# A four-block transformer kernel: bf16 queries by ScalarE, two single turns of maxima, an earlier load, idle matmuls at the first score, new order tables

## The reference, cut to what matters

```python
x = L0(x): x + g*attn(ada_ln(x)), self attention with rotary q and k and a mask
           x + g*attn(ada_ln(x), context), key mask
           x + g*mlp(ada_ln(x))            # 128 -> 512 -> 128, gelu
x = L1(x): x + attn(ada_ln(x), ada_ln(context))
x = L2(x): x + g*attn(ada_ln(x)); x + attn(ln(x), context); x + g*mlp(ada_ln(x))
x = L3(x): q = ln(x) @ Wq; evidence = softmax(q k / sqrt(128)) v   # one head
           three experts and a gate over [ln(x), evidence, anchor]
# attention: 16 heads of 8 channels
s = einsum('bqhd,bkhd->bhqk', q, k) / sqrt(8); a = softmax(s); o = a @ v
```

## Time and profile before

| | |
|---|---|
| runs, median | 585.58 us (580.8 to 586.85) |
| profiled execution, its time | 584.01 us |
| its span, first to last instruction | 581.9 us |
| mean granted TensorE clock | 0.974 |
| TensorE busy | 541.6 us, 93% |
| TensorE weight loads busy | 336.1 us, 58% |
| VectorE busy | 384.7 us, 66% |
| ScalarE busy | 319.7 us, 55% |
| GpSimd busy | 336.2 us, 58% |

### The profile page before, as it was taken

The page is one execution under the profiler, slowest core; times in us unless marked ns, Lnnn a source line. Parts: engine busy times, 40 slices in busy tenths (PEclk is TensorE's granted clock), DMA queues, the critical chain, the costliest instruction groups (busy, mean ns, idle before and its releaser), DMA issues.

```text
span 581.9 us, 17488 instructions
## 1 busy us (share of the span) xinstructions
PE 541.6 (93%) x7121; PEld 336.1 (58%) x7126; DVE 384.7 (66%) x1062; ACT 319.7 (55%) x523; POOL 336.2 (58%) x424
## 2 busy tenths in 40 slices
PE   7799889999899999999999989998999999997996
PEld 3354445556455675556565645655668647775565
DVE  4847788976878577867688568789727513635124
ACT  2004256454655856674757575665746669444671
POOL 3372874582979757886688785778747302343000
PEclk9757899999999999999999999999999999999999
DMA  7810200010100010001000000000000000000000
GB/s 254 289 51 4 75 21 3 4 37 2 37 3 21 3 37 2 21 2 38 2 13 10 20 20 3 3 7 15 5 17 2 2 2 1 19 19 0 1 2 37
DMA packets 17818, 16.07 MB, mean 28 GB/s; under 512 B 4333, under 2 KB 15863, under 8 KB 17483
## 3 DMA queue, kind: packets, MB, share of 16 engines
q1 hardware_dynamic: 16875, 10.82, 6.3%
q10 hardware_dynamic: 864, 4.13, 1.9%
HBM read 13.85 MB, written 1.09 MB: 26 GB/s over the span
## 4 chain that ended last, share of the span: by engine, by line
PE 61%; DVE 8%; ACT 6%; issue 5%; POOL 2%; POOLq 0%; DVEq 0%; ACTq 0%
PE ring L1074 16%; PE ring L1086 13%; PE big L1175 10%; PE ring L1208 8%; DVE mhl L891 3%; ACT P L655 3%; PE ring L1151 3%; PE big L1192 2%; PE ring L1096 2%; PE ring L1081 2%; DVE bst L827 1%; ACT hT L633 1%; POOL xn L547 1%; DVE oT L932 1%; PE ring L1140 1%
## 5 line engine op out<-in xcount | busy, mean ns | idle before, releaser
L891 DVE TENSOR_REDUCE mhl<-ring 128x4 bf16<-128x308 f32 (+1 forms) x320 | 163.9, 549 | 39.3 <-PE ring L1151 30.5
L655 ACT ACTIVATE P<-big 77x1024 f32<-77x1024 f32 (+1 forms) x128 | 124.6, 1019 | 104.0 <-PE big L1192 103.4
L547 POOL TENSOR_SCALAR xn<-x,mv,rstd 128x128 f32<-128x128 f32 x124 | 100.2, 822 | 3.2
L562 POOL TENSOR_TENSOR kbm<-kT,hm 128x308 bf16<-128x308 f32 (+1 forms) x80 | 69.2, 870 | 56.3 <-DVE kT L875 22.2
L575 POOL TENSOR_TENSOR qm<-qT,hm 128x512 f32<-128x512 f32 x80 | 83.7, 1051 | 25.3 <-PE big L1192 21.0
L1175 PE MATMUL big<-qm,kT 32*77 32x512 f32 (+1 forms) x640 | 91.5, 630 | 3.3 <-ACT P L655 2.8
L1074 PE MATMUL ring<-hT,W 128*128 128x512 f32 x176 | 90.0, 616 | 4.2 <-ACT hT L633 3.0
L1208 PE MATMUL ring<-P,Vp 77*32 77x128 f32 (+1 forms) x2560 | 86.5, 275 | 4.3 <-DVE mhl L891 1.2
L1208 PEld LDWEIGHTS ring<-P,Vp 77*32 77x32 f32 (+1 forms) x2560 | 65.6, 109 | 25.2 <-issue 15.6
L633 ACT ACTIVATE hT<-ring,tab 128x128 f32<-128x128 f32 x96 | 36.1, 460 | 52.7 <-PE ring L1096 52.3
L1086 PEld LDWEIGHTS ring<-W,hid 128*128 128x128 f32 x480 | 57.4, 192 | 2.8 <-issue 2.0
(11 more groups left out here) (169 smaller groups left out, 734.8 us busy)
## 6 DMA issues: line engine op xcount, KB each, us to landing
gring<-gate_rows SPq DMA_DIRECT2D x20, 256.0 KB, 3.5
W<-in_w ACTq DMA_DIRECT2D x1, 2624.0 KB, 15.0
hid<-in_ws SPq DMA_DIRECT2D x1, 1536.0 KB, 12.2
x<-in_x SPq DMA_DIRECT2D x4, 256.0 KB, 4.6
out<-x SPq DMA_DIRECT2D x4, 256.0 KB, 2.0
W<-in_w ACTq DMA_DIRECT2D x1, 768.0 KB, 6.8
ctxT<-in_ctxT SPq DMA_DIRECT2D x4, 154.0 KB
ctx<-in_ctx SPq DMA_DIRECT2D x4, 154.0 KB
```

The lines of the kernel that those rows point to most:

```text
L547: i = nc.gpsimd.tensor_scalar(dst[0:t, b, :], src[0:t, b, :], mv[s][0:t, o, b, 0:1], rstd[s][0:t, o, 1, b:b + 1], ALU.subtract, ALU.mult)
L562: nc.gpsimd.tensor_tensor(kbm[:, j % 2, :, 0:kw], k.broadcast_to([128, 4, kw]), mask.broadcast_to([128, 4, kw]), ALU.mult).then_inc(kbm_re ...
L655: nc.scalar.activation(P[0:kw, j % 2, 8 * half:8 * half + 8, :], big[0:kw, 2 * half:2 * half + 2, :].rearrange("p g (h q) -> p (g h) q", h=4),
L891: v.tensor_reduce(mhl[:, j // 2 % 2, c:c + 4], at(item)[:, 0:4 * kw].rearrange("p (h k) -> p h k", h=4), AX, ALU.max).then_inc(free(item), 1)
```

## The change

- `p{a}:qc:s` leaves VectorE. For attentions 1 to 4, ScalarE's item `p{a}:q:s` now makes two copies from the projection's bank: first `qb` in bf16, then `qT` in f32, which frees the bank. For attention 0 ScalarE gets an item `p0:qc:s`, a copy of `qT` to `qb` behind the rotation.
- `SINGLE = 2`: the maxima of jobs 0 and 1 are turned each by itself (`tu:0`, `tu:1`), those of later jobs in pairs as before. The halves of `mhl` and `mt` go by the number of the turn.
- x of group 1 is loaded behind the identity, ahead of the masks, and its statistics stand ahead of the first rotation.
- `PE_IDLE`: 20 idle matmuls at `s:0:0`, 11 instead of 21 at the first transposes, none at `p0:v:0`, others at items of jobs 0 to 5.
- All four tables are new; the modulation columns are spread among the first scores, the signs stand ahead of the first normalisation, and elsewhere items move by a place or two.

```diff
-u:g0:0=1 u:g1:0=1 s:0:1=1 s:0:3=1 s:1:3=1 s:2:2=2 l0:t:0=21 p0:v:0=5 p0:k:1=1
+u:mc:0=1 s:0:0=20 s:0:3=4 s:1:2=3 s:2:0=1 s:3:0=3 s:3:1=1 s:3:3=1 av:3=1 s:5:0=1 s:5:2=2 l0:t:0=11 p0:v:1=1
...
 PE_ORDER = program("""
-l0:t:0 p0:q:0 p0:k:0 p0:v:0 s:0:0 s:0:1 s:0:2 s:0:3 s:1:0 s:1:1 u:ma:0 u:mb:0 u:mc:0 u:mods:0 s:1:2 s:1:3 s:2:0 st:0
-s:2:1 s:2:2 tu:0 l0:t:1 su:0 s:2:3 s:3:0 s:3:1 p0:q:1 u:g0:0 p0:k:1 s:3:2 s:3:3 st:1 u:g1:0 su:1 av:0 p0:v:1 tu:2 st:2
...
+l0:t:0 p0:q:0 p0:k:0 p0:v:0 s:0:0 s:0:1 s:0:2 u:ma:0 s:0:3 s:1:0 s:1:1 s:1:2 u:mb:0 tu:0 s:1:3 s:2:0 st:0 su:0 s:2:1
+s:2:2 u:mc:0 l0:t:1 tu:1 u:mods:0 st:1 su:1 s:2:3 s:3:0 s:3:1 p0:q:1 p0:k:1 st:2 s:3:2 s:3:3 av:0 p0:v:1 u:g0:0 tu:2
+su:2 av:1 u:g1:0 s:4:0 s:4:1 st:3 su:3 s:4:2 s:4:3 s:5:0 s:5:1 av:2 av:3 s:5:2 s:5:3 u:bias:0 tu:4 st:4 su:4 s:6:0
...
 DVE_ORDER = program("""
-l0:stat:0 first:0 l0:a:0 first:1 first:2 p0:qa:0 p0:ka:0 p0:k:0 p0:q:0 p0:qc:0 p0:v:0 mx:0:0 mx:0:1 mx:0:2 mx:0:3
-mx:1:0 mx:1:1 l0:stat:1 u:mc:0 u:ma:0 u:mb:0 u:mods:0 mx:1:2 l0:stat:2 mx:1:3 mx:2:0 mx:2:1 tr:0 mx:2:2 mx:2:3 mx:3:0
...
+l0:stat:0 first:1 l0:a:0 first:0 first:2 l0:stat:1 p0:qa:0 p0:ka:0 p0:k:0 p0:q:0 p0:v:0 mx:0:0 mx:0:1 u:ma:0 mx:0:2
+mx:0:3 mx:1:0 mx:1:1 mx:1:2 tr:0 u:mb:0 l0:stat:2 mx:1:3 mx:2:0 mx:2:1 mx:2:2 l4:stat:0 u:mc:0 tr:1 u:mods:0 mx:2:3
...
 ACT_ORDER = program("""
-l0:t:0 l0:t:1 ex:0:0 ex:0:1 ex:1:0 ex:1:1 ex:2:0 ex:2:1 ex:3:0 ex:3:1 ex:4:0 p1:k:0 ex:4:1 ex:5:0 ex:5:1 l0:t:2 l1:t:0
...
+l0:t:0 p0:qc:0 ex:0:0 ex:0:1 l0:t:1 ex:1:0 ex:1:1 p0:qc:1 ex:2:0 ex:2:1 ex:3:0 ex:3:1 ex:4:0 ex:4:1 l0:t:2 p1:k:0
...
 POOL_ORDER = program("""
-l0:r:0 kb:0 kb:1 kb:2 qm:0 l0:a:1 qm:1 kb:3 l0:a:2 qm:2 kb:4 kb:5 qm:3 l4:a:0 qm:4 kb:6 nm:0 kb:7 qm:5 l0:a:3 qm:6
...
+l0:r:0 kb:0 qm:0 kb:1 qm:1 kb:2 l0:a:1 kb:3 l0:a:2 qm:2 kb:4 kb:5 qm:3 kb:6 qm:4 nm:0 qm:5 kb:7 qm:6 l0:a:3 l1:a:0
...
+SINGLE = 2
...
 def pair_of(j):
 
-    return j - j % 2
+    return j if j < SINGLE else j - j % 2
+
+
+def pair_last(j):
+    return j if j < SINGLE else pair_of(j) + 1
...
+TURNS = list(dict.fromkeys(pair_of(j) for j in range(JOBS)))
+
+
+def turn_of(j):
+    return TURNS.index(pair_of(j))
...
             sp.dma_start(ident[:], ident_in).then_inc(ident_ld, 16)
+            sp.dma_start(xs[1][:], x_in[:, GB:2 * GB, :]).then_inc(x_in_s[1], 16)
             for c in range(4):
...
-            for s in range(1, NS):
+            for s in range(2, NS):
                 sp.dma_start(xs[s][:], x_in[:, s * GB:(s + 1) * GB, :]).then_inc(x_in_s[s], 16)
...
             def project(a, s, part):
                 A, item = ATT[a], (f"p{a}", part, s)
+                if part == "qc":
+                    act.wait_ge(rope_q[s], 1)
+                    nc.scalar.activation(qb[s][:], qT[s][:], ACT.Identity).then_inc(qb_ready[s], 1)
+                    return
+                if part == "q":
+
+                    full(act, item)
+                    kw = {"bias": c_(A["bq"])} if A["bq"] else {}
+                    nc.scalar.activation(qb[s][:], at(item), ACT.Identity, **kw).then_inc(qb_ready[s], 1)
                 dst, n, bias = (qT, N, A["bq"]) if part == "q" else (kT, GB * A["kw"], A["bk"])
...
-            def cast(a, s):
-                if a == 0:
-                    dve.wait_ge(rope_q[s], 1)
-                else:
-                    taken(dve, (f"p{a}", "q", s))
-                v.tensor_copy(qb[s][:], qT[s][:]).then_inc(qb_ready[s], 1)
...
-                if g == 0 and j >= 4:
+                if g == 0 and turn_of(j) >= 2:
 
-                    full(dve, ("tu", pair_of(j) - 4))
+                    full(dve, ("tu", TURNS[turn_of(j) - 2]))
...
-                taken(pe, ("s", j + 1, 3))
+                taken(pe, ("s", pair_last(j), 3))
```

More of the change, by code:

```diff
@@ L104 @@
[L104 to L108, removed]
@@ new lines @@
+s:37:2 st:35 su:35 s:37:3 s:38:0 av:34 tu:36 s:38:1 s:38:2 st:36 su:36 av:35 s:38:3 s:39:0 l1:t:3 s:39:1 s:39:2 st:37
+s:39:3 su:37 av:36 p1:q:3 av:37 l4:t:2 tu:38 st:38 s:40:0 s:40:1 s:40:2 su:38 s:40:3 s:41:0 o2:y:1 l2:t:2 s:41:1
+s:41:2 st:39 s:41:3 su:39 av:38 m0:h0:2 m0:h1:2 m0:h2:2 m0:h3:2 p1:v:3 tu:40 av:39 m0:y:2 st:40 s:42:0 s:42:1 su:40
+s:42:2 o3:y:0 p4:k:0 p2:k:2 st:41 s:42:3 su:41 s:43:0 s:43:1 s:43:2 s:43:3 av:40 l3:t:2 tu:42 st:42 su:42 p2:q:2
+p2:v:2 av:41 s:44:0 s:44:1 l5:t:1 s:44:2 s:44:3 st:43 s:45:0 su:43 s:45:1 s:45:2 s:45:3 av:42 l6:t:0 tu:44 av:43
@@ L194 @@
-x3:r2:2 x3:e0:2 x3:r2:3 x3:e1:2 x3:e0:3 x3:e1:3 x3:e2:3 x3:y:3 x3:e2:2 x3:y:2
+l0:stat:0 first:1 l0:a:0 first:0 first:2 l0:stat:1 p0:qa:0 p0:ka:0 p0:k:0 p0:q:0 p0:v:0 mx:0:0 mx:0:1 u:ma:0 mx:0:2
+mx:0:3 mx:1:0 mx:1:1 mx:1:2 tr:0 u:mb:0 l0:stat:2 mx:1:3 mx:2:0 mx:2:1 mx:2:2 l4:stat:0 u:mc:0 tr:1 u:mods:0 mx:2:3
+mx:3:0 p0:qa:1 mx:3:1 p0:ka:1 mx:3:2 p0:k:1 mx:3:3 p0:q:1 tr:2 t1:0 p0:v:1 u:g0:0 l0:stat:3 u:g1:0 t1:1 mx:4:0 mx:4:1
+mx:4:2 mx:4:3 mx:5:0 t1:2 mx:5:1 t1:3 nr:0 mx:5:2 mx:5:3 nt:0 tr:4 u:bias:0 mx:6:0 mx:6:1 o0:y:0 l1:stat:0 mx:6:2
@@ new lines @@
+mx:6:3 mx:7:0 mx:7:1 t1:4 mx:7:2 mx:7:3 t1:5 tr:6 l4:stat:2 l4:stat:3 p1:v:0 l4:stat:1 mx:8:0 mx:8:1 mx:8:2 mx:8:3
+mx:9:0 t1:6 mx:9:1 mx:9:2 mx:9:3 t1:7 mx:10:0 tr:8 mx:10:1 mx:10:2 mx:10:3 nr:1 mx:11:0 mx:11:1 mx:11:2 p0:ka:2
+mx:11:3 p0:k:2 tr:10 t1:8 p0:qa:2 p0:q:2 t1:9 p0:v:2 nt:1 mx:12:0 mx:12:1 mx:12:2 mx:12:3 mx:13:0 t1:10 mx:13:1
+mx:13:2 t1:11 mx:13:3 nr:2 mx:14:0 tr:12 o0:y:1 nt:2 l1:stat:1 mx:14:1 mx:14:2 o1:y:0 mx:14:3 mx:15:0 mx:15:1
+l2:stat:0 t1:12 mx:15:2 mx:15:3 tr:14 t1:13 mx:16:0 mx:16:1 mx:16:2 mx:16:3 p1:v:1 mx:17:0 mx:17:1 mx:17:2 mx:17:3
@@ L234 @@
+qm:73 l7:a:1 nm:17 qm:74 kb:75 kb:76 l6:a:3 kb:77 qm:75 qm:76 l8:a:0 qm:77 kb:78 kb:79 qm:78 l8:a:1 nm:18 qm:79 l7:a:2
+nm:19 l7:a:3 l8:a:2 l8:a:3
 """)
@@ L895, in turn @@
                 item = ("tu", j)
-                if j >= 4:
-                    dve.wait_ge(st_full, 2 * (j - 3) + 2)
+                if turn_of(j) >= 2:
+                    dve.wait_ge(st_full, 2 * pair_last(TURNS[turn_of(j) - 2]) + 2)
                 full(dve, item)
-                v.tensor_copy(mt[:, j // 2 % 2, :], at(item).bitcast(BF16)[:, 0:T]).then_inc(free(item), 1)
+                v.tensor_copy(mt[:, turn_of(j) % 2, :], at(item).bitcast(BF16)[:, 0:T]).then_inc(free(item), 1)
             def unload(j):
@@ L1026, in _ @@
                     norm(int(st[1:]), item[2])
-                elif part == "qc":
-                    cast(int(st[1:]), item[2])
                 elif st == "p0" and part in ("q", "k"):
@@ L1180, in turn @@
                 take(item)
-                taken(pe, ("s", j + 1, 3))
+                taken(pe, ("s", pair_last(j), 3))
                 hold(pe)
-                give(item, nc.tensor.transpose(at(item).bitcast(BF16)[:, 0:T], mhl[:, j // 2 % 2], identb[:]))
+                give(item, nc.tensor.transpose(at(item).bitcast(BF16)[:, 0:T], mhl[:, turn_of(j) % 2], identb[:]))
             def subtract(j):
```

216 lines of the change are left out of this document (103 added, 113 removed).

## The result

The changed kernel took 582.78 us (median; 575.94 to 590.86) against 585.03 of the kernel before in the same sessions: ratio 0.9933, 95% interval 0.9905 to 0.9961, 0.4 to 1.0% faster; the two medians alone give 0.9962. The forecast was 579.5, its range (571 to 590) held the time, and the sum was 2.7 times too large (-6.0 for -2.25). The range was wide enough to hold "no change" too, so that it held is no evidence for the sum. Runs of one kernel lie up to 3.5% apart here; ratios and intervals leave out runs over 1.5% above the fastest of their kernel, while medians are of all runs, so the ratio of a widely spread kernel is better than its medians say, and the ratio of the medians is given beside it.

A forecast was written before the change was run, and what follows sets the result against it. TensorE was taken to set the pace, at half clock from 22.4 us for 27.3 us, and later as limit in name. Terms -1.3 + 6.0 - 5.7 - 1.0 - 1.2 - 2.8 = -6.0 us gave 579.5, range 571 to 590.

The forecast's parts named there:

- VectorE's idle time behind TensorE: First maximum to job 4: full clock halves VectorE's wait (-6.2), one cast less there (-0.8); -7.0 us.
- the dip: Second half-clock stretch, 66.8 to 70.2 us, costing 1.7 us; taken as gone with chance 0.7, -1.2 us.
- The burst: Twenty idle matmuls at the first score follow the wait, a plain delay partly at half clock; +6.0 us (4.5 to 8.9).
- head: Up to the first scores: transposes 0.8 us earlier, bf16 queries 0.5 us sooner by ScalarE's copy; -1.3 us.
- other idle matmuls: First maximum to job 5: 11 further idle matmuls, half of their 2.5 us beside VectorE's work; +1.3 us.
- single turns: Jobs 0 and 1: first exponentials begin after four maxima instead of eight; -1.0 us (+0.4 to -3).
- other casts: Sixteen later query casts leave VectorE for ScalarE, one operation instead of two before scores; -2.8 us (+1.5 to -6).
- I take nothing: Head: earlier load of group 1's x priced at zero, up to +1 us if modulation weights are late.
- First jobs: First four jobs: clock regained, -7.0, against +1.3 for further idle matmuls; sum -5.7 us.
- the tables: Rest of the new tables, moving single items by one or two places: taken at nothing, with +-3 us.
- rival (c): First jobs: burst runs at half clock behind the wait and doesn't hold the clock; slower, +7.9, 593.5 us; chance 0.15.
- Given back: Head, burst and halved waits as forecast, -1.0, nothing later since the block's chain and TensorE's load set the rest; 584.5, chance 0.25.

The follow-up runs named there:

- e4: Changed kernel without the twenty idle matmuls at the first score; 587.58 us.
- e6: Kernel before, with its own tables, casts and loads, plus twenty idle matmuls at the first score, issued ahead of the key and query waits; 582.15 us.
- e2: Changed kernel with x of group 1 loaded behind the masks and its statistics behind the second maximum on VectorE; 591.17 us.
- e9: e3 with jobs 0 and 1 turned as one pair again (SINGLE = 0); 590.35 us.
- e5: Changed kernel with the copies to bf16 queries back on VectorE at their old places; 591.95 us.
- e3: Changed kernel with idle matmuls issued ahead of the waits for keys and queries in all score items; 579.03 us.
- e8: e3 plus nine idle matmuls in the last stage; 585.03 us.
- e10: e3 with 26 idle matmuls ahead and 20 more sprinkled through the first two jobs and modulation columns; 582.20 us.
- e1: Changed kernel with x of group 1 loaded behind the masks, nothing else; 590.09 us.
- e7: Changed kernel with the burst ahead of the waits, x of group 1 loaded where before loaded it, its statistics behind the second maximum; 588.09 us.
- e11: The same kernel as e3, run again; 584.73 us.
- e12: e3 with nine more idle matmuls: three each before ma and mb, one before mc, two ahead; 579.92 us.

## Why the forecast came out as it did

The mechanism held: the clock over the first jobs came back, and that pays for a burst that itself is plain delay. e4, which takes the burst out, and e6, which puts one into the old kernel, show it. The first score was forecast 4.7 us late (-1.3 + 6.0) and in the profiled run came 10.3 late; what follows was forecast at -7.9 to the end of the first block (-5.7, -1.0, -1.2) and measured -7.6 there (first score to first milestone: 51.3 before, 43.7 after).

Over all runs, by the two parts of a time: the terms that are mostly clock (-7.0, VectorE's idle time behind TensorE, and -1.2, the dip) make -8.2, and the clock gave some -9.4. The burst was forecast at 6.0 and cost 6.2 of work. What failed is the rest, forecast at -3.8 (head -1.3, other idle matmuls +1.3, single turns -1.0, other casts -2.8): it came to 5.6 - 6.2 = -0.6. That is the largest part of what the sum was off by, as far as work is good to a us or two. By its steps:

- **Head, -1.3.** The transposes were better than forecast (-1.3 for -0.8) and ScalarE's copy right (0.63 us for 0.65, from a source in SBUF). But "I take nothing" for the early x failed. I moved x past the masks on SyncE's queue (about twenty places, not "six or so") and priced 0.9 us of bandwidth. The masks went out 0.48 us later, and in the profiled run VectorE waited 6.9 us. The queries were 3.9 us late there instead of 1.3 early. That profile is a bad case: in the eight other profiles with this order of loads the wait was 0.9 to 7.0 us, 3.0 in the middle. And it is worth less than it looks: e2, without the wait, had 0.8 us less work. I had written that masks are needed only behind signs and tables; with those moved ahead of the normalisation, that is early.
- **Burst, +6.0.** Measured 6.41 in the trace and 6.2 of work (e4). Its reason held too: it follows the wait (8.54 us, where I had 4.8), starts at half clock and ends at full.
- **First jobs, -5.7, single turns -1.0, dip -1.2.** Sum right in one profile each, see above. The 66.8 dip is gone, in e6 with the old tables too. The single turns alone were not settled (e9).
- **Sixteen other casts, -2.8.** Mis-sized. From the second milestone to the last the old tables take 410.8 us (before) and 410.4 (e6), the changed ones, in the eight profiles where no dip falls in, 409.8 to 410.2: 0.3 to 1.0 us for casts and tables together. From the first milestone to the second it is 40.4 and 40.1 against 38.5 to 38.6. Those 1.4 to 1.9 us are the tables', forecast at nothing, and not the casts': e5, with the casts back on VectorE, takes 38.5 as well. VectorE lost 11.7 us of casts and 12.1 us of waiting for ScalarE, and the idle time came back as waits on TensorE: those for L1164 after 75 us (L1151 before) went from 30.5 to 37.1 us, those for the averages (L1221, before L1208) from 13.4 to 23.7. TensorE at 94 to 98 of each 100 us, which I had called a limit "in name", is the likely bound; no run tests it by itself. Waits of VectorE after 75 us (us in total, times, longest), before and then after:

```profile
DVE mhl L891 <- PE ring L1151: 30.5, 43, 3.6
...
DVE avt L908 <- PE ring L1208: 13.4, 22, 3.4
```

```profile
DVE mhl L906 <- PE ring L1164: 37.1, 45, 6.4
...
DVE avt L923 <- PE ring L1221: 23.7, 30, 3.6
```

e5 says something else at first sight, 4.9 us of work for the casts. But those tables were written without casts on VectorE; in tables that had them the same casts cost nothing visible (e6, work 568.5). A part undone inside tables made for it prices the misfit too. That reading is argued and not shown: the run that would decide, ScalarE's copies in the old tables, wasn't made.

- **Rivals.** The burst at half clock throughout (rival (c)) did not come, the clock was back by 30 us. Its "more full-array work in one piece than stands before 49.7" holds only for what follows the fall: 21 such matmuls stand at 7.16. "Given back", 584.5, lay nearer to the 582.78 than the forecast did: the steady stage behaved as it described.

The Trainium skill, "TensorE: Matmul & The Clock Gate", part 1, has it that activity releases the throttle. The windows of e3 and e8 show both answers for one list of instructions and the same busy share, 0.74 and 1.00; with e10's 26 further idle matmuls all four runs kept it. The rule points the right way but, by busy time, decides nothing here.

## What to carry to other kernels

Idle matmuls ahead of the wait that they are to fill cost less than behind it, where they are plain delay, in part at half clock: 1.5 to 2.5 us of work here instead of 6.2. Behind it they seemed to hold the clock better (18.6 us at half clock against 26.1), so measure both. When a load is issued earlier, ask what it pushes past another queue's bulk transfers, not what its bytes cost. Read the granted clock of every run beside its time, and compare time with the clock's share taken off before saying that an edit helped: here that share moved runs of one kernel (e3) by 17 us, nearly eight times the effect of the whole change.

## What the runs showed of the hardware

**Small loads against bulk loads of another queue.** The last mask is issued by SyncE at 6.84 us with x ahead of it and at 6.36 without; ScalarE's queue issues three weight loads, 2.6 MB the largest, at 5.87 to 6.43, whenever its turn comes. VectorE's wait for the masks in the profiled runs, by how long the last mask goes out behind the weights (us):

```
behind   kernel    wait for masks
0.05     e2        none
0.10     before    none
0.41     e5        1.2
0.42     e6        none
0.45     e1, e7    0.8, 1.0
0.58     e4        0.9
0.58     e8        3.3
0.66     e10       2.7
0.70     e11       3.3
0.78     e12       4.9
0.79     e3        2.4
0.92     after     6.9
0.96     e9        7.0
```

Half a microsecond of issue time became up to 7 us of landing time for 16 KB each. The five kernels without x ahead (before, e1, e2, e6, e7) all lie at 0.45 or less, but among the nine with it the trend is the same. One profiled run stands for each kernel, so this is a trend and not a law.

**One program, many clocks.** e3, e8 and e11 are one list of instructions up to 520 us; their eighteen runs go from 571.7 us at a clock of 0.995 to 592.7 at 0.960, median 581.8. What tips it in a run was not settled: e9's profile has a hole of 6.04 us ahead of the fall, e7's one of 2.64, e3 falls at 28 us after a hole of 1.42 at 20, and e8 with one of 0.60 keeps its clock. One difference stands earlier: in e8, e11 and e12, which keep the clock but for a dip of 3 us in e11, it was at half from 12 to 14 us on and came back at 17 to 19, before the first score; in e3, e6 and e9, where it falls at 25 to 28 and stays low for some 20 us, it had been full from the start. But e7 had the early dip too and fell at 27 behind its hole. No run tested whether the dip matters.
